# A graph kernel: the sort's schedule in the first 45 units, its exchanges partly in PSUM, and single rows in every block

## The chip, the cores and the metric

One core of a Trainium2 chip runs the whole program. The metric is device time in microseconds, from one launch to its end. TensorE (PE) multiplies, VectorE (DVE), ScalarE (ACT) and GpSimd (POOL) work element by element, SyncE (SP) only issues transfers. POOL also issues the indirect transfers, in which each of 128 partitions fetches or writes one row at an address that it holds itself.

## What is computed

The input is `x`, 12500 nodes of 256 features, with two graphs on it. With `ln` for the layer norm over features:

```
x1  = x  + (segment_sum(ln(x)[src] * edge_weight, dst) @ W.T + b)     # 200000 edges, sorted by dst
h   = ln(x1) @ W_gat                      # 16 numbers per node: 4 heads x 4 experts
att = softmax over the edges into each node of leaky_relu(a_src[src] + a_dst[dst])
                                          # 131072 unsorted edges and a loop per node
scores = mean over heads of ln(segment_sum(h[src] * att) + b_gat) * gamma + beta
w   = softmax over the best 2 of the 4 experts, 0 for the others
out = x1 + sum over experts e of w[e] * (gelu(ln(x1) @ W1[e] + b1[e]) @ W2[e] + b2[e])
```

## The kernel before

All is float32. The kernel has four parts: `layernorm_and_plan` (the normalised rows and a plan of steps), `weighted_sums`, `attention_and_experts` and `combine`. The change touches the second and the third.

**weighted_sums** (lines 504 to 1128). The 200000 edges stand in 1563 columns of 128, four columns to a group, 391 groups. POOL fetches the source rows of a group with four indirect gathers (L712) into one of the 16 slots of the ring `rows`; before it refills a slot it waits until TensorE has done the last step on the group that lies there. A step (L881) multiplies one group with one-hot matrices that VectorE writes (L938 and L942, into a ring of 4 steps), and adds to the sums of one tile of 128 nodes in PSUM. There are 488 steps: one for each group, and one more for each tile end inside a group. The destinations are dense at low node numbers (`dst` is 12500 times the square of a uniform number), so early steps seldom end a tile and late ones often do. At a tile's end TensorE runs `stages` (L859 to L873), and ScalarE takes the results out of PSUM.

Beside the steps VectorE sorts the 131072 edges of the second graph by destination, and counts them. The order is written out by hand: the loop over steps is cut into 60 units of 8 steps, and between the loops of two units stand pieces of the sort (`sort_at`), histogram pieces (`hist_at`), and on TensorE the histogram's matmuls and transposes of the keys (`TURN_AT`).
- The sort is bitonic, with keys of 128 partitions by 1024 columns. Inside a partition it is done by `exchange`: the smaller and the larger of the elements that differ in one bit of the column number, in two operations from one SBUF buffer into another (L987, L988). There are 153 exchanges in 24 stretches (pieces 0 to 23). Between stretches 9 to 23 TensorE transposes the keys into the PSUM tensor `turned`, and VectorE copies them out (L1000).
- A histogram piece takes 32 compares on VectorE (L1059) and 16 matmuls on TensorE. There are 64. The buffers hold two, so that VectorE waits for the matmuls of the piece two before.

The table gives the last unit that holds each thing, before and after the change. It follows from the table of numbers in the code:

| | before | after |
|---|---|---|
| first transpose of keys | unit 15 | unit 11 |
| last exchange, end of the sort | unit 51 | unit 45 |
| last histogram piece | unit 49 | unit 42 |
| units with no sort and no histogram behind the last transpose, to unit 59 | 52 to 59 | 46 to 59 |

After the last step the terms of the nodes are computed (L1093 to L1107), and POOL spreads the destinations' terms to the first edge of each node (L502), 28 of 98 tiles here and the others in the next part.

**attention_and_experts** (lines 1130 to 1618). TensorE runs the experts' matmuls (L1369, L1380) for 49 pairs of tiles. Beside them the attention runs over the 1024 sorted edge columns in eight blocks, the last one of 44 columns and the others of 140. A column of a block is fetched by one indirect gather on POOL (L1286), except its last two columns in the first seven blocks: these SP fetches with 256 transfers of one row each (`single_rows`, L1253), whose addresses it reads out of SBUF (`ask`, L1239). VectorE computes a block between the work of fixed pairs, and the last block behind them.

## Time and profile before

| | us |
|---|---|
| three timed runs | 3705.07, 3705.21, 3710.14 (median 3705.21) |
| the profiled execution | 3709.83 |
| its span in the trace | 3708.0 |

The span lies 1.8 us under the device time of the same execution, and that execution is 4.6 us above the median of the three.

| engine | busy us | share |
|---|---|---|
| PE | 3033.7 | 82% |
| POOL | 2700.9 | 73% |
| DVE | 2035.0 | 55% |
| ACT | 819.2 | 22% |

Shares over the whole span hide that the stages have different limits. `weighted_sums` lasts until about 2115 us, `attention_and_experts` from there to about 3531 us, and `combine` takes the rest. Each must be read by itself.

### The profile page before, as it was taken

To read this page: it belongs to the slowest core of one execution; us is meant where nothing else is said; L and a number is where in the kernel's file an instruction comes from. 1 tells how busy PE (TensorE), PEld (TensorE's weight loads), DVE (VectorE), ACT (ScalarE), POOL (GpSimd) and SP (SyncE) were. 2 spreads that over 40 slices of the span, in tenths; PEclk is the share of its full clock that TensorE was granted. 3 is DMA by queue.
4 is the path that set the end of the run, shared out by engine and by line. 5 is a ranking of instruction groups with operands and counts; after the bars stand their busy time and mean duration, and the time that the engine had idled before them with its cause. 6 is when DMAs were issued, how large, how long until landed. Compare 5 with 4: busy or idle time off the path is not lost. (4 is left out here: it accounts for less than half of the span.)

```text
span 3708.0 us, 65908 instructions
## 1 busy us (share of the span) xinstructions
PE 3033.7 (82%) x13893; PEld 2476.2 (67%) x13894; DVE 2035.0 (55%) x6854; ACT 819.2 (22%) x2321; POOL 2700.9 (73%) x2803
## 2 busy tenths in 40 slices
PE   1666667667777777887899799999999999999748
PEld 1454445555565555665677588888888888888637
DVE  8875566576667767666664322353434343343567
ACT  6300000100111111111122222222332223222247
POOL 6677777777777777777677477777777777777573
PEclk6788887887888878788899899999999999999979
DMA  9633333434444444444344122232322222223279
GB/s 346 209 115 105 108 108 110 115 113 114 117 118 114 118 118 120 118 124 118 106 125 133 51 72 54 53 112 63 75 57 73 54 72 60 73 54 75 65 281 381
DMA packets 280932, 426.20 MB, mean 115 GB/s; under 512 B 63672, under 2 KB 214499, under 8 KB 279651
## 3 DMA queue, kind: packets, MB, share of 16 engines
q0 software_dynamic: 113760, 216.95, 23.2%
q1 hardware_dynamic: 68911, 114.88, 8.5%
q10 hardware_dynamic: 98004, 91.50, 7.6%
q8 instruction: 93, 1.52, 0.2%
q14 instruction: 164, 1.34, 0.1%
HBM read 317.12 MB, written 105.98 MB: 114 GB/s over the span
## 5 line engine op out<-in xcount | busy, mean ns | idle before, releaser
L712 POOL DMA_INDIRECT rows<-feats,src_t x1500 | 1459.6, 973 | 484.0 <-issue 453.5
L881 PE MATMUL node_sums<-rows,ys_ahead 128*128 x3904 | 1063.5, 432 | 479.7 <-DVE ys_ahead L942 244.8
L881 PEld LDWEIGHTS node_sums<-rows,ys_ahead 128*128 128x128 f32 x3904 | 817.0, 216 | 683.9 <-issue 550.2
L1286 POOL DMA_INDIRECT got<-row_dram,src_sorted x1010 | 977.2, 968 | 308.1 <-issue 308.1
L1369 PE MATMUL d_hidden<-d_yt,w 128*128 128x256 f32 x3136 | 711.2, 380 | 0.8 <-DVE d_yt L1455 0.8
L1380 PE MATMUL d_expert<-w,hid 128*128 128x256 f32 x3136 | 708.7, 379 | 0.0
L1380 PEld LDWEIGHTS d_expert<-w,hid 128*128 128x128 f32 x3136 | 595.8, 190 | 81.0
L1369 PEld LDWEIGHTS d_hidden<-d_yt,w 128*128 128x128 f32 x3136 | 593.7, 191 | 80.3 <-DVE d_yt L1455 1.2
L1432 DVE TENSOR_TENSOR yo<-d_expert,x_and_b 128x512 f32<-128x512 f32 x196 | 135.5, 691 | 839.8 <-PE d_expert L1380 832.2
L942 DVE TENSOR_SCALAR ys_ahead<-iota,rel,ew_t 128x128 f32<-128x128 f32 x1952 | 557.2, 361 | 66.4 <-DVE rel L938 3.8
L1313 ACT ACTIVATE hid<-d_hidden,b1c 128x256 f32<-128x256 f32 x784 | 324.4, 471 | 982.5 <-PE d_hidden L1369 793.4
L771 ACT COPY edge_plan<-node_sums 128x256 f32<-128x256 f32 x98 | 36.5, 373 | 1665.0 <-PE sums_and_xc_turned L873 1665.0
L938 DVE TENSOR_SCALAR rel<-dst_t,step_base 128x4 f32 x488 | 125.7, 258 | 473.2 <-PE node_sums L881 330.3
L1059 DVE TENSOR_SCALAR ys_ahead<-iota_b,hist_columns 128x128 bf16<-128x128 bf16 (+1 forms) x2048 | 333.4, 281 | 2.3
L502 POOL DMA_INDIRECT adst_first<-node_dst,first_pos x98 | 97.0, 990 | 66.3 <-DVEq L1106 36.7
L1712 POOL DMA_INDIRECT edge_plan<-state_dram,last_pos x98 | 96.0, 980 | 31.8 <-issue 29.6
L869 PE MATMUL x_product<-edge_plan 128*128 128x256 f32 x400 | 114.2, 412 | 0.0
L1783 PE MATMUL f_sum<-ys,gate_diagonals 128*128 128x256 f32 x384 | 89.4, 393 | 22.7 <-issue 11.6
L1783 PEld LDWEIGHTS f_sum<-ys,gate_diagonals 128*128 128x128 f32 x384 | 74.6, 197 | 37.1 <-issue 26.4
L1055 DVE CAST hist_columns<-ys_ahead 128x16 f32<-128x16 bf16 x128 | 17.3, 186 | 147.3 <-PE counts L893 140.2
L869 PEld LDWEIGHTS x_product<-edge_plan 128*128 128x128 f32 x400 | 83.6, 209 | 13.7
L346 POOL DMA_INDIRECT rows<-in_x,src_t x64 | 61.9, 967 | 34.1 <-issue 19.2
(303 smaller groups left out, 2315.0 us busy)
## 6 DMA issues: line engine op xcount, KB each, us to landing
y_dram<-yo ACTq DMA_DIRECT2D x196, 256.0 KB
ys<-y_dram SPq DMA_DIRECT2D x36, 1024.0 KB, 9.2
got<-row_dram SPq DMA_DIRECT2D x1792, 0.1 KB
rows<-feats,src_t POOLq DMA_INDIRECT x1500
got<-row_dram,src_sorted POOLq DMA_INDIRECT x1010, 2.4
ys_ahead<-y_dram SPq DMA_DIRECT2D x13, 1024.0 KB, 9.1
x_dram<-edge_plan ACTq DMA_DIRECT2D x98, 128.0 KB
d_x<-x_dram ACTq DMA_DIRECT2D x49, 256.0 KB
```

What stands on the lines that cost most here:

```text
L712: pool.indirect_dma_start(rows[:, g % RING, j, :], None, feats, bass.IndirectOffsetOnAxis(ap=m.src_t[:, g * GT + j:g * GT + j + 1], axis=0 ...
L869: t = pe.matmul(psX[:, 0:FEAT], sums_t[:, k * P:(k + 1) * P], w_t[:, k, :], start=False, stop=(k == HALVES - 1))
L881: t = pe.matmul(psA[:, ds(((code >> 1) & 1) * 512, FEAT)], hot[:, r, j, :], rows[:, ds((code >> 2) & (RING - 1), 1), j, :], start=False, s ...
L938: v.tensor_scalar(rel[:, r, :], m.dst_t[:, ds(g * GT, GT)], m.step_base[:, ds(s, 1)], None, ALU.subtract).then_inc(s_rel, 1)
L942: t = v.tensor_scalar(hot[:, r, j, :], m.iota[:], rel[:, r, j:j + 1], m.ew_t[:, ds(g * GT + j, 1)], ALU.is_equal, ALU.mult)
L1059: c.inc(v.tensor_scalar(t[:, q % 2, j, :], iota_b[:, 0:wide], col[:, q % 2, n, j:j + 1], None, ALU.is_equal))
L1286: pool.indirect_dma_start(got[:, k, j, 0:ROWF], None, m.row_dram, bass.IndirectOffsetOnAxis(ap=m.src_sorted[:, BEGIN[b] + j:BEGIN[b] + j + ...
L1313: t = act.activation(hid[:, e % 2, 2 * q + f, :], psL[(e % 2) * 2 + q][:, f, :], ACT.Gelu, bias=b1c[:, e, 2 * q + f:2 * q + f + 1])
L1369: t = pe.matmul(psL[(e % 2) * 2 + q][:, f, :], w1[:, h, e, (2 * q + f) * P:(2 * q + f + 1) * P], yt[:, k, h, :], start=(h == 0), stop=(h = ...
L1380: q = pe.matmul(psO[e % 2][:, t, :], hid[:, e % 2, f, t * P:(t + 1) * P], w2[:, f, e, :], start=(f == 0), stop=(f == FB - 1))
L1432: v.tensor_tensor(yo[:, e, :, :], psO[e % 2][:], xb[:, e, :, :], ALU.add).then_inc(s_yo, 1)
L1783: q = pe.matmul(psum[j % SUMS][:, t, :], diag[:, j % DIAGS, t, e, :], y_of(i)[:, t, e, :], start=(e == 0), stop=(e == EXPERTS - 1))
```

## The change

Three edits.

1. The table of the sort's pieces and of the histogram's. A stretch of up to 7 exchanges is no longer cut in two (before: up to 5), short stretches share a unit up to 6 exchanges, and a unit takes two histogram pieces whenever its exchanges are at most 4 (before: only in a unit with a transpose).
2. `exchange` makes four operations of half the size where it made two. The elements whose next bit is one are written to the PSUM tensor `turned` instead of SBUF, so that the next exchange has one input in SBUF and one in PSUM. Only the first exchange of each of the 24 stretches has both inputs in SBUF. The exchange of bit 0 stays at two operations and writes SBUF only.
3. The last block too gets its last two columns from SP. SP fetches the single rows of block 0 before it waits for the 98 spread tiles and loads `adst`.

```diff
-            half = bits_of(n) if bits_of(n) <= 5 else (bits_of(n) + 1) // 2
+            half = bits_of(n) if bits_of(n) <= 7 else (bits_of(n) + 1) // 2
...
-            u += n >= 9
+            u += 2 * (n >= 9)
...
-            more = min(HPIECES - q, 2 if n in TURN_AT else 1)
+            more = min(HPIECES - q, 1 if sum(z - a for _, a, z in sort_at.get(n, [])) > 4 else 2)
...
+            def upper(bit):
+
+                n = bit % 2 * (GCOLS // 2)
+                return psT[:, n:n + GCOLS // 2].rearrange("p (a w) -> p a w", w=1 << bit)
+
-            def exchange(buf, bit):
+            def exchange(buf, bit, first):
+
                 to = 1 if buf == 2 else 1 - buf
                 a = key[buf].rearrange("p (a h w) -> p a h w", h=2, w=1 << bit)
                 o = key[to].rearrange("p (a h w) -> p a h w", h=2, w=1 << bit)
-                c.inc(v.tensor_tensor(o[:, :, 0, :], a[:, :, 0, :], a[:, :, 1, :], ALU.min))
-                c.done(v.tensor_tensor(o[:, :, 1, :], a[:, :, 0, :], a[:, :, 1, :], ALU.max))
+                x, y = a[:, :, 0, :], a[:, :, 1, :] if first else upper(bit)
+                if bit == 0:
+                    c.inc(v.tensor_tensor(o[:, :, 0, :], x, y, ALU.min))
+                    c.done(v.tensor_tensor(o[:, :, 1, :], x, y, ALU.max))
+                    return to
+                half = 1 << (bit - 1)
+                u = upper(bit - 1).rearrange("p (a h) w -> p a h w", h=2)
+                for side, op in ((0, ALU.min), (1, ALU.max)):
+                    c.inc(v.tensor_tensor(o[:, :, side, 0:half], x[:, :, 0:half], y[:, :, 0:half], op))
+                    c.inc(v.tensor_tensor(u[:, :, side, :], x[:, :, half:2 * half], y[:, :, half:2 * half], op))
+                v.wait_ge(s_s, c.n)
                 return to
...
-        single = lambda b: SINGLE if b < BLOCKS - 1 else 0
...
             ask(0)
+            single_rows(0)
             sp.wait_ge(m.s_sc, 16 * TILES)
             sp.dma_start(adst[:], m.adst_first[0:GEDGES, :].rearrange("(p j) h -> p j h", p=P)).then_inc(s_ad, 16)
-            single_rows(0)
             for b in range(BLOCKS):
-                if b + 1 < BLOCKS - 1:
+                if b + 1 < BLOCKS:
                     ask(b + 1)
                     single_rows(b + 1)
```

VectorE at the end of the sort, before: these operations stand behind the steps of unit 51. `seg_keep` and `src_sorted` are the two key buffers in SBUF, and the numbers are the partitions and the shape of the output.

```order
L987 TENSOR_TENSOR src_sorted<-seg_keep 128x128x4
L988 TENSOR_TENSOR src_sorted<-seg_keep 128x128x4
L987 TENSOR_TENSOR seg_keep<-src_sorted 128x256x2
L988 TENSOR_TENSOR seg_keep<-src_sorted 128x256x2
L987 TENSOR_TENSOR src_sorted<-seg_keep 128x512
L988 TENSOR_TENSOR src_sorted<-seg_keep 128x512
L1019 TENSOR_SCALAR seg_keep<-src_sorted 128x1024
```

After the change the same exchanges stand behind the steps of unit 45. `turned` is the PSUM tensor.

```order
L1002 TENSOR_TENSOR src_sorted<-seg_keep,turned 128x128x2
L1003 TENSOR_TENSOR turned<-seg_keep,turned 128x128x2
L1002 TENSOR_TENSOR src_sorted<-seg_keep,turned 128x128x2
L1003 TENSOR_TENSOR turned<-seg_keep,turned 128x128x2
L1002 TENSOR_TENSOR seg_keep<-src_sorted,turned 128x256
L1003 TENSOR_TENSOR turned<-src_sorted,turned 128x256
L1002 TENSOR_TENSOR seg_keep<-src_sorted,turned 128x256
L1003 TENSOR_TENSOR turned<-src_sorted,turned 128x256
L996 TENSOR_TENSOR src_sorted<-seg_keep,turned 128x512
L997 TENSOR_TENSOR src_sorted<-seg_keep,turned 128x512
L1035 TENSOR_SCALAR seg_keep<-src_sorted 128x1024
```

Two operations over 512 elements have become four over 256, except the last exchange, and each has one input in SBUF and one in PSUM. In all VectorE gets 258 operations more, two for each of 129 exchanges.

SP at the start of `attention_and_experts`, before: the index load, the load of `adst`, and then the first single rows.

```order
L1239 DMA edge_plan<-src_sorted 1x128x2
L1259 DMA adst<-adst_first 128x4096
L1248 TENSOR_LOAD edge_plan
L1253 ISA
L1253 DMA got<-row_dram 1x20
```

After the change the single rows of block 0 (now L1268) stand between the two, and `adst` (now L1275) is followed by the index load of block 1:

```order
L1268 ISA
L1268 DMA got<-row_dram 1x20
L1275 DMA adst<-adst_first 128x4096
L1254 DMA edge_plan<-src_sorted 1x128x2
L1263 TENSOR_LOAD edge_plan
```

The 256 transfers have moved ahead of the load of `adst`.

## Rows read from the trace of the kernel before

**Rows 1.** The page's costliest groups: busy us, mean ns of one, idle before.
```profile
L712 POOL DMA_INDIRECT rows<-feats,src_t x1500 | 1459.6, 973 | 484.0 <-issue 453.5
...
L1059 DVE TENSOR_SCALAR ys_ahead<-iota_b,hist_columns 128x128 bf16<-128x128 bf16 (+1 forms) x2048 | 333.4, 281 | 2.3
```

**Rows 2.** Windows of L712 alone, POOL's gathers: busy us (x instructions), clock, DMA.
```profile
0.00:1682.00 1682.00, 1195.11 (x1228) 0.83 0.45 133
```

**Rows 3.** Windows of L938 alone, one operation of VectorE per step.
```profile
0.00:1682.00 1682.00, 96.99 (x373) 0.83 0.45 133
1890.00:2087.00 197.00, 16.41 (x64) 1.00 0.38 112
```

**Rows 4.** Windows of L859 alone, four matmuls per tile end.
```profile
0.00:1682.00 1682.00, 41.70 (x244) 35.69 (x244) 0.83 0.45 133
1890.00:2087.00 197.00, 13.05 (x85) 11.01 (x85) 1.00 0.38 112
```

**Rows 5.** Waits of PE from 220 to 1000 us: total us, times, longest.
```profile
PE node_sums L881 <- SPq L696: 163.2, 69, 7.9
```

**Rows 6.** Waits of PE from 1000 to 1890 us.
```profile
PE node_sums L881 <- DVE ys_ahead L942: 140.9, 19, 8.5
PE node_sums L881 <- SPq L696: 50.0, 9, 8.4
```

**Rows 7.** Waits of PE from 1890 to 2090 us, the whole answer.
```profile
PE node_sums L881 <- issue: 0.6, 2, 0.4
```

**Rows 8.** Waits of POOL from 1730 to 1900 us.
```profile
POOL rows L712 <- PE node_sums L881: 18.3, 8, 6.8
```

**Rows 9.** Windows of L712 over the 38 stretches of exchanges, sum of all.
```profile
sum 205.30, POOL 159.84; mean POOL 4.21
```

**Rows 10.** Timeline of DVE, inputs in SBUF and PSUM (e_turn).
```profile
2123.87 0.41 DVE L1439 TENSOR_TENSOR x_and_b<-d_x,e_turn 128x256 f32<-128x256 f32 x1
2124.31 0.42 DVE L1441 TENSOR_TENSOR x_and_b<-d_x,e_turn 128x256 f32<-128x256 f32 x1
2124.65 0.41 DVE L1439 TENSOR_TENSOR x_and_b<-d_x,e_turn 128x256 f32<-128x256 f32 x1
```

**Rows 11.** Timeline of POOL in the experts' part.
```profile
3442.59 0.94 POOL L1286 DMA_INDIRECT got<-row_dram,src_sorted  x1 [0.30 <-issue]
3443.84 1.15 POOL L1286 DMA_INDIRECT got<-row_dram,src_sorted  x1 [0.30 <-issue]
```

**Rows 12.** Timeline of DVE at the same place.
```profile
3442.56 0.69 DVE L1432 TENSOR_TENSOR yo<-d_expert,x_and_b 128x512 f32<-128x512 f32 x1 [4.84 <-PE d_expert L1380]
...
3443.74 0.42 DVE L1441 TENSOR_TENSOR x_and_b<-d_x,b2r 128x256 f32<-128x256 f32 x1
```

**Rows 13.** Timeline of POOL at the end of the gathers.
```profile
2045.57 0.95 POOL L712 DMA_INDIRECT rows<-feats,src_t  x1 [0.30 <-issue]
2083.25 1.78 POOL L502 DMA_INDIRECT adst_first<-node_dst,first_pos  x1 [36.73 <-DVEq L1106]
```

**Rows 14.** Timeline of PE at the last step.
```profile
2083.07 3.72 PE L881 MATMUL node_sums<-rows,ys_ahead 128*128 x16
```

**Rows 15.** Windows of all engines in the experts' part: PE, PEld, DVE, ACT, POOL.
```profile
2200.00:2300.00 100.00, 100.00 (x471) 88.05 (x470) 27.08 (x55) 23.19 (x56) 75.90 (x80) 1.00 0.30 74
```

**Rows 16.** Timeline of SP at the start of the experts' part.
```profile
2116.73 0.55 SPq L1239 DMA_DIRECT2D edge_plan<-src_sorted  x1
2212.29 0.33 SPq L1259 DMA_DIRECT2D adst<-adst_first  x1
2213.62 134.46 SPq L1253 DMA_DIRECT2D got<-row_dram  x256
```

**Rows 17.** Line L1467, the first use of adst: ns min/median/max, first and last start.
```profile
L1467 DVE TENSOR_TENSOR_SCAN adst<-seg_keep,adst x4: 2283/2285/2293, 2335.3 to 2356.2; 128x1024 f32<-128x1024 f32 x4
```

**Rows 18.** Timeline of DVE where the last block begins.
```profile
3507.74 0.18 DVE L1478 TENSOR_SCALAR limit<-seg_keep 128x44 f32<-128x44 f32 x1 [0.23 <-DVE last_state L1515]
```

More of the change, by code:

```diff
@@ L608, in weighted_sums @@
         for n in range(PIECES):
-            half = bits_of(n) if bits_of(n) <= 5 else (bits_of(n) + 1) // 2
+            half = bits_of(n) if bits_of(n) <= 7 else (bits_of(n) + 1) // 2
             for a in range(0, bits_of(n), half):
-                sort_at[u] = (n, a, min(a + half, bits_of(n)))
-                u += 1
-            last_of.append(u - 1)
-            u += n >= 9
+                if sort_at.get(u) and sum(z - y for _, y, z in sort_at[u]) + min(half, bits_of(n) - a) > 6:
+                    u += 1
+                sort_at.setdefault(u, []).append((n, a, min(a + half, bits_of(n))))
+            last_of.append(u)
+            u += 2 * (n >= 9)
         TURN_AT = {last_of[n] + 1: n - 9 for n in range(9, PIECES - 1)}
@@ L993, in columns @@
                 for bit in range(bits_of(n) - 1 - a, bits_of(n) - 1 - z, -1):
-                    buf = exchange(buf, bit)
+                    buf = exchange(buf, bit, first=bit == bits_of(n) - 1)
                 return buf
@@ L1123, in _ @@
                     sort_init()
-                if n in sort_at:
-                    buf = sort_piece(*sort_at[n], buf)
+                for piece in sort_at.get(n, []):
+                    buf = sort_piece(*piece, buf)
                 if n == SORTED:
@@ L1206, in attention_and_experts @@
         size = lambda b: BEGIN[b + 1] - BEGIN[b]
-        single = lambda b: SINGLE if b < BLOCKS - 1 else 0
-        in_quarter = lambda b, q: max(0, min(size(b) - single(b), (q + 1) * QUARTER) - q * QUARTER)
+        in_quarter = lambda b, q: max(0, min(size(b) - SINGLE, (q + 1) * QUARTER) - q * QUARTER)
         rows_of = lambda b: got[:, b % NBUF, 0:size(b), :]
@@ L1284, in _ @@
                     pool.wait_ge(s_kept[k], b // NBUF * 16)
-                for j in range(size(b) - single(b)):
+                for j in range(size(b) - SINGLE):
                     pool.indirect_dma_start(got[:, k, j, 0:ROWF], None, m.row_dram,
@@ L1475, in maxima @@
                         v.wait_ge(s_got[b % NBUF][q], 16 * sum(in_quarter(a, q) for a in range(b % NBUF, b + 1, NBUF)))
-                if single(b):
-                    v.wait_ge(s_single, 16 * (1 + SINGLE * P) * (b + 1))
+                v.wait_ge(s_single, 16 * (1 + SINGLE * P) * (b + 1))
                 c.done(v.tensor_scalar(limit[:, 0:n], m.seg_keep[:, j], 2 * BIG, -BIG, ALU.mult, ALU.add))
```

## Prediction

> **What bounds the kernel now.** I read the 40 slices first, then windows over each part. In the experts' part TensorE is busy all the time, at the full clock (2.4 GHz), while POOL is at 76% and VectorE at 27% [rows 15]. No edit takes work from TensorE there, so I looked for the gain in `weighted_sums`, which ends near 2115 us.
>
> There two chains run side by side. POOL must issue 1500 gathers. One takes 973 ns and 0.30 us of issue, 1.27 us together, or 5.1 us for a group of four [rows 1]. VectorE and TensorE must work off the groups. Up to 1000 us TensorE waits 163 us for rows [rows 5]: POOL is the slower chain. From 1000 to 1890 us it waits only 50 us for rows but 141 us for one-hot matrices that VectorE, busy with the sort and the histogram, delivers late [rows 6]. So here the pair falls behind. At 1682 us, where unit 46 begins, POOL has issued (64+1228)/4 = 323 groups (the 64 gathers of the first ring included), and VectorE has begun 373 steps at 244/4 = 61 tile ends, which is group 311 [rows 2 to 4]. The lead is 12 of the 16 slots. Soon after, the ring is full: POOL waits 18.3 us in all for TensorE between 1730 and 1900 us, in 8 waits [rows 8].
>
> From 1890 us on there is neither sort nor histogram, and TensorE waits for nothing [rows 7]. The last gather ends at 2046.5 us, the last step at 2086.8 us, 40 us later; POOL sits idle for 36.7 us until it may spread the terms [rows 13, 14]. So the pair's work sets the end, and everything after moves with it.
>
> **The cost of an exchange.** Now 153 exchanges fill 205.3 us [rows 9], 1.34 us each. Four operations of 256 elements with one input in PSUM: the trace has such operations, and the next one starts 0.34 us later where nothing is waited for, and 0.44 us later behind a wait [rows 10]. Three by 0.34 plus 0.44 is 1.46 us, so 0.12 us more per exchange, and 15 us of VectorE time over 129 exchanges. The lower end is 1.34, as now. No row shows VectorE writing PSUM. The upper end is four operations that each take as long as one of 512 elements now, 0.67 us: 2.68 us. I take 1.46, from the rows with the same size and the same inputs; that a write to PSUM costs what one to SBUF does is my assumption.
>
> The Trainium skill speaks against this edit. Its page VectorE: DVE Perf Modes, section The TRN2 errata, gives a fixed 58 cycles for an operation from SBUF and 120 for one from PSUM, 65 ns more. By that an exchange would take 1.7 us and the forecast would be some 8 us later. The rows do not show that difference.
>
> **What an exchange does to POOL.** The 38 stretches of exchanges last 205.3 us, in which POOL is busy 159.8 us [rows 9]. The 45.5 us left, at 0.30 us a gather, are some 150 gathers of 1.07 us, where an undisturbed gather lasts 0.95 and the next starts after 1.25 us (3442.59 to 3443.84 [rows 11]), which would make 164. So the exchanges hold POOL up by 14 gathers, 18 us. In the experts' part the same is seen in single operations: the gather that starts beside `yo`, which reads PSUM and SBUF, takes 0.94 us, and the one beside `x_and_b<-d_x,b2r`, which reads SBUF twice, takes 1.15 us [rows 11, 12]. With 129 of 153 exchanges no longer reading SBUF twice I take back 129/153 of 18, 15 us. The bounds are 0 and 18 us.
>
> Here the Trainium skill has another view. Its page SBUF — State Buffer, section Who interferes with whom, says that `tensor_tensor` takes only the pair's read interface while descriptor generation needs the write interface (it marks this as inferred). By that the 15 us are zero. The gathers of 1.07 us contradict it here.
>
> **The pair's chain, after.** Up to unit 27 (near 1050 us) TensorE waits for rows anyway, and the denser units use those 163 us; I cost that at nothing. Without this cover the ring would be full earlier, and each further us of work would be one at the end. From there to unit 46 the new table has 62 exchanges instead of 55, and 23 histogram pieces instead of 25. In VectorE time: 62 by 1.46 less 55 by 1.34 is +17 us. Two histogram pieces fewer, at 333.4/64 = 5.2 us [rows 1] and about 1 us around them, -12 us. The end of the sort, nine or so operations over 1024 elements, and two more copies out of PSUM: an estimate of +13 us, scaled from the 512-element operations. Together +18 us. TensorE's steps run beside part of VectorE's work, so I put half on the path, +9: unit 46 starts at 1691 us (0 to 18 bound it: 1682 to 1700).
>
> From there 80 groups remain, 311 to 390, with no sort and no histogram. Their price is what the end of the trace shows: from 1890 us to the last step 64 one-hot sets are begun, and TensorE has two or three steps still to do at the start; less 85/4 = 21 tile ends [rows 3, 4] that is about 46 groups in 197 us, 4.3 us a group. 80 by 4.3 is 344 us, so the last step ends at 2035 us.
>
> **POOL's chain, after.** It has to be checked, because it may be the later of the two. The last gather ended at 2046.5. Less 15 us (exchanges) and less 16 us (the 18.3 of waits, less 8 by 0.30 of ordinary issue) it ends at 2015 us. Landing, a step and the tile ends around it add 6 to 10 us: 2023 us. The pair's chain is later, and the two terms on POOL do not add to the gain; they are what lets the pair run on without a wait.
>
> So the last step moves from 2086.8 to 2035, -52 us. The tail behind it (four tile ends, the last terms, the spreads) is unchanged.
>
> **The edits at nothing.** SP loads `adst` behind 256 single rows, 134.5 us [rows 16]. Before, the load went out at 2212.3 because it waits for the 98 spreads; now it goes out some 136 us after the first index load at 2116.7, so at 2253 us on the old scale, 40 us later. Its first use is at 2335.3 [rows 17]. About 70 us of cover are left. What is queued behind it on SP, the next index load and single rows, comes no later than before. In the last block POOL saves two gathers, 2.5 us, but VectorE begins that block right behind its own last operation, idle for 0.23 us [rows 18], so nothing is won; SP's 256 rows for it go out beside the pairs before. Zero for both.
>
> **Sum.** Profiled span 3708.0 - 52 = 3656 us, and with the 1.8 us around it 3658. The median stands 4.6 us under the profiled execution: 3653 us, 1.4% faster. A difference of 0.2% (7.4 us) is what a measurement of this kernel can tell from none.
>
> **Rivals.**
> - *The ring fills in the middle.* If the added work falls wholly on the path, or TensorE's clock, 0.83 on the mean up to 1682 us [rows 2], stays low in the denser units, the ring is full before unit 46 and POOL stands as it did at 1730 us. The lead of 12 slots of 16 at 1682 us speaks for it: 4 slots are 20 us. The price is +9 for the half that I left off the path and 10 to 20 us of POOL's standing. 3675 us.
> - *POOL is the bound.* If the pair gets through the last 14 units at less than 4.3 us a group (units 46 to 50 end fewer tiles than the last ones), the floor of 2023 us counts: -64 us, 3641 us. Against it: in supply-bound stretches the clock was lower, and the pair slower.
> - *PSUM brings nothing to POOL.* Then POOL's chain ends 15 us later, at 2038, about level with the pair's, and each disturbs the other a little: 3660 us. [rows 11, 12] speak against it.
> - *Writing PSUM is dear* (the slow side). An exchange of 2.68 us adds 1.22 us to each of 62 exchanges from 1050 us on, all on the path once the pair is the bound: +76 us against -52, so 3705 + 24 = 3729 us. It decides from 2.3 us an exchange on, where 62 times the excess eats the 52. Only the missing row speaks for it, and that ScalarE and TensorE also use PSUM then.
>
> **Chances.** Forecast 0.50 (3645 to 3667); ring fills 0.17; POOL bound 0.12; PSUM without gain 0.08; PSUM dear 0.07; the rest, such as a new wait in the order of transposes and histogram pieces, 0.06, half of it slower or same. The range reaches from the POOL bound, 3638, to a full ring at its dearest, 3690. Faster 0.87, within 0.2% 0.05, slower 0.08.
>
> **What would show it.** Exchanges: operations of 0.41 us that follow each other by 0.34. POOL: gathers beside them at 0.95 us, and no waits for TensorE around 1750 us. The pair: a lead of 12 slots or more at the start of unit 46, near 1690 us, shrinking to a few, so that the last step follows the last gather by some 20 us and not 40. The experts' part: as long as before, TensorE at 100%. The forecast is wrong if the lead reaches 16 before unit 40, if an exchange takes over 1.6 us, or if VectorE waits at the first use of `adst`.

## The result, and the profile after

| | us |
|---|---|
| before, four runs | 3705.07 to 3710.14, median 3706.56 |
| after, four runs | 3660.9 to 3672.25, median 3666.07 |
| ratio | 0.989, 95% interval 0.9869 to 0.9911 |
| profiled execution after | 3672.25, span 3670.3, mean clock 0.897 |

The change makes the kernel 1.1% faster. The forecast was 3653 us with a range from 3638 to 3690: right in its sign and inside the range, 13 us too low.

Two lines of the page after: the gathers, and the operation of VectorE with which each histogram piece begins (busy us, mean ns of one, idle before, and what ended most of it).

```profile
L713 POOL DMA_INDIRECT rows<-feats,src_t x1500 | 1438.5, 959 | 495.9 <-issue 442.3
...
L1071 DVE CAST hist_columns<-ys_ahead 128x16 f32<-128x16 bf16 x128 | 17.9, 196 | 146.6 <-PE counts L894 137.6
```

Against [rows 1] the 1500 gathers last 21.1 us less (1459.6 to 1438.5, 973 to 959 ns), but the idle time ahead of them is 11.9 us longer (484.0 to 495.9). The difference of the two, 9.2 us, is nearly all of how much earlier the last gather ends: 2037.1 instead of 2046.5 us. The experts' matmuls take 380 ns, as before, and from 2200 to 2300 us TensorE is busy for all of the 100 us, as in [rows 15].

How far the pair of VectorE and TensorE stands behind POOL is counted as in [rows 2 to 4]: windows over L713 (gathers), L939 (one per step) and L860 (four matmuls per tile end), of the kernel after, from the start to the beginning of units 27, 42 and 46.

```profile
0.00:1054.00 1054.00, 715.57 (x745) 0.79 0.47 142
0.00:1579.00 1579.00, 1100.43 (x1148) 0.81 0.45 133
0.00:1699.00 1699.00, 1184.10 (x1235) 0.81 0.44 132
```

```profile
0.00:1054.00 1054.00, 55.55 (x221) 0.79 0.47 142
0.00:1579.00 1579.00, 85.97 (x340) 0.81 0.45 133
0.00:1699.00 1699.00, 94.13 (x373) 0.81 0.44 132
```

```profile
0.00:1054.00 1054.00, 15.68 (x96) 13.32 (x96) 0.79 0.47 142
0.00:1579.00 1579.00, 35.79 (x212) 30.57 (x212) 0.81 0.45 133
0.00:1699.00 1699.00, 40.74 (x244) 34.74 (x244) 0.81 0.44 132
```

At 1054 us: (64+745)/4 = 202 groups issued, 221 - 96/4 = 197 begun, a lead of 5. The same count for the kernel before, at its unit 27, has two rows (L712, L938) and the same 24 tile ends:

```profile
0.00:1047.00 1047.00, 711.59 (x732) 0.81 0.47 141
```

```profile
0.00:1047.00 1047.00, 56.90 (x220) 0.81 0.47 141
```

(64+732)/4 = 199 less 196 is 3. At 1579 us after: 303 issued, 340 - 53 = 287 begun. The lead is 16, the ring is full. At 1699 us it is 325 - 312 = 13. The same count on [rows 2 to 4] gives 323 - 312 = 11 at unit 46 before; the 12 of the prediction takes the group by its number, which starts at 0.

The windows end where a unit begins, so they also give the time of each stretch (the last two rows are read from their traces in the same way):

| us | to unit 27 | units 27 to 45 | unit 46 to the end of the last step | sum |
|---|---|---|---|---|
| before | 1047 | 635 | 405 | 2087 |
| forecast | 1047 | 644 | 344 | 2035 |
| after | 1054 | 645 | 350 | 2049 |
| table alone (h1_schedule) | 1052 | 647 | 349 | 2048 |
| histogram earlier (f1_hist_early) | 1072 | 583 | 368 | 2023 |

Waits of TensorE from 220 to 1000 us, and from 1000 to 1890 us (total, times, longest):

```profile
PE node_sums L882 <- DVE ys_ahead L943: 182.8, 21, 14.0
PE node_sums L882 <- SPq L697: 91.8, 22, 13.9
```

```profile
PE node_sums L882 <- DVE ys_ahead L943: 155.2, 22, 13.8
PE node_sums L882 <- SPq L697: 11.3, 4, 7.9
```

By these lines the waits for rows before 1000 us fell from 163.2 [rows 5] to 91.8 us, and those for VectorE rose to 182.8 us. Before the change the same stretch had for VectorE:

```profile
PE node_sums L881 <- DVE ys_ahead L942: 82.0, 14, 8.4
```

From 1000 to 1890 us they stand at 11.3 us for rows and 155.2 for VectorE, against 50.0 and 140.9 [rows 6].

These lines put a wait down to the semaphore that moved last before it, and here that is wrong for the long ones. A step really waits for rows in the first of these two places, and for VectorE in the second:

```profile
472.46 0.94 POOL L713 DMA_INDIRECT rows<-feats,src_t  x1 [0.30 <-issue]
475.71 0.48 PE L882 MATMUL node_sums<-rows,ys_ahead 128*128 x1 [2.97 <-SPq L697]
```

```profile
351.46 1.11 DVE L943 TENSOR_SCALAR ys_ahead<-iota,rel,ew_t 128x128 f32<-128x128 f32 x4
353.19 1.22 PE L882 MATMUL node_sums<-rows,ys_ahead 128*128 x2 [13.94 <-SPq L697]
```

At 475.71 TensorE starts 2.3 us behind the last gather of the step's group, and the one-hot matrices have been ready for 7 us. At 353.19 it starts 0.6 us behind the last one-hot matrix, and the rows were fetched 22 us before. Sorted by these two distances, step by step, the waits for rows from 220 to 1000 us are 149 us before and 33 us after, and those for VectorE 93 and 240 us. From 1000 to 1890 us the waits for rows are 3 us before and none after. So up to unit 27 the denser units used up most of the time in which TensorE had waited for rows, and the pair of VectorE and TensorE sets the pace behind it in both kernels.

Waits of POOL for TensorE, first in all, then the two longest, each in the brackets of the gather that it held up:

```profile
POOL rows L713 <- PE node_sums L882: 53.5, 48, 9.6
```

```profile
1485.83 0.94 POOL L713 DMA_INDIRECT rows<-feats,src_t  x1 [9.60 <-PE node_sums L882]
...
1523.03 0.94 POOL L713 DMA_INDIRECT rows<-feats,src_t  x1 [7.12 <-PE node_sums L882]
```

It was 30.5 us in all before, and the part of it in [rows 8] lay behind 1730 us. The first wait of the ring lasts 9 to 10 us in both kernels, but the page before puts it down to issue: behind 200 us the sums are 29.3 us before and 43.7 us after. Now POOL stands again and again from 1476 us, the start of the wait of 9.6 us, up to 1620 us, in units 39 to 43. It waits for TensorE, and VectorE may be four steps ahead of TensorE, so POOL stands already at a lead of 12 or so, counted as above.

The waits of TensorE from unit 46 to the last step (1699 to 2050 us), and the one long one among them:

```profile
PE node_sums L882 <- DVE ys_ahead L943: 9.8, 2, 9.5
PE node_sums L882 <- SPq L697: 0.2, 1, 0.2
```

```profile
1700.82 3.78 PE L882 MATMUL node_sums<-rows,ys_ahead 128*128 x8 [9.54 <-DVE ys_ahead L943]
```

This wait is for the last exchanges and the end of the sort on VectorE. Behind it TensorE runs without a pause to the last step. It waits 0.2 us for rows: the pair still sets the end, and not POOL.

The end of the first part, on POOL and on TensorE:

```profile
2036.19 0.95 POOL L713 DMA_INDIRECT rows<-feats,src_t  x1 [0.30 <-issue]
2044.98 1.77 POOL L502 DMA_INDIRECT adst_first<-node_dst,first_pos  x1 [7.84 <-DVEq L1122]
```

```profile
2044.95 3.72 PE L882 MATMUL node_sums<-rows,ys_ahead 128*128 x16
```

Against [rows 13, 14], the last gather is 9 us earlier, the last step ends at 2048.7 instead of 2086.8 us, 38 us earlier, and POOL is idle for 7.8 instead of 36.7 us before it spreads. That is the whole gain: from the end of the last step to the end of the span it takes 1621.2 us before and 1621.6 after.

| us | last gather ends | last step ends | from there to the end of the span |
|---|---|---|---|
| before | 2046.5 | 2086.8 | 1621.2 |
| after | 2037.1 | 2048.7 | 1621.6 |
| table alone (h1_schedule) | 2037.8 | 2047.5 | 1619.0 |
| histogram earlier (f1_hist_early) | 2017.5 | 2023.3 | 1622.7 |

VectorE in three exchanges that follow each other, after (start, duration):

```profile
238.28 0.42 DVE L1002 TENSOR_TENSOR src_sorted<-seg_keep,turned 128x256 f32<-128x256 f32 x1
238.61 0.42 DVE L1003 TENSOR_TENSOR turned<-seg_keep,turned 128x256 f32<-128x256 f32 x1
...
239.28 0.42 DVE L1003 TENSOR_TENSOR turned<-seg_keep,turned 128x256 f32<-128x256 f32 x1
239.73 0.63 DVE L1002 TENSOR_TENSOR seg_keep<-src_sorted,turned 128x256 f32<-128x256 f32 x1
240.26 0.62 DVE L1003 TENSOR_TENSOR turned<-src_sorted,turned 128x256 f32<-128x256 f32 x1
...
241.29 0.62 DVE L1003 TENSOR_TENSOR turned<-src_sorted,turned 128x256 f32<-128x256 f32 x1
241.94 0.69 DVE L996 TENSOR_TENSOR src_sorted<-seg_keep,turned 128x512 f32<-128x512 f32 x1
```

Two operations of another exchange of bit 1, the first of its stretch, with both inputs in SBUF:

```profile
140.83 0.63 DVE L1002 TENSOR_TENSOR seg_keep<-src_sorted 128x256 f32<-128x256 f32 x1
141.36 0.62 DVE L1003 TENSOR_TENSOR turned<-src_sorted 128x256 f32<-128x256 f32 x1
```

And a gather of POOL beside the first exchange:

```profile
238.94 0.95 POOL L713 DMA_INDIRECT rows<-feats,src_t  x1 [0.30 <-issue]
```

The first four operations are an exchange as forecast, 0.42 us each and 0.33 us apart, and a gather beside them takes 0.95 us; the next follows by 1.25. The next four are the exchange of bit 1. Each of its operations takes single elements, every fourth one of a key buffer in SBUF and every second one in PSUM. Each takes 0.62 us and starts 0.52 us after the last: 2.2 us for the exchange. The row at 140.83 shows that PSUM is not the reason: it neither reads nor writes it and takes as long. The last row of the first list is bit 0, two operations of 512 elements, every second one of a key buffer, and takes the same 0.69 us as in the kernel before.

### The profile page after: what moved, and what is told of

It reads as the page before. It is cut to its first block and busy times, and to the rows that moved or that the text cites. A ratio compares the mean times of both kernels' runs of the same rounds, so it can differ in the third digit from the quotient of the medians.

```text
span 3670.3 us, 66961 instructions
## 1 busy us (share of the span) xinstructions
PE 2976.7 (81%) x13893; PEld 2447.2 (67%) x13894; DVE 2067.3 (56%) x7112; ACT 817.7 (22%) x2321; POOL 2677.2 (73%) x2801
## 5 line engine op out<-in xcount | busy, mean ns | idle before, releaser
L713 POOL DMA_INDIRECT rows<-feats,src_t x1500 | 1438.5, 959 | 495.9 <-issue 442.3
L882 PE MATMUL node_sums<-rows,ys_ahead 128*128 x3904 | 1019.7, 420 | 499.1 <-DVE ys_ahead L943 377.3
L882 PEld LDWEIGHTS node_sums<-rows,ys_ahead 128*128 128x128 f32 x3904 | 796.8, 210 | 683.3 <-issue 555.4
L939 DVE TENSOR_SCALAR rel<-dst_t,step_base 128x4 f32 x488 | 122.1, 250 | 403.1 <-PE node_sums L882 267.5
L502 POOL DMA_INDIRECT adst_first<-node_dst,first_pos x98 | 96.3, 983 | 37.4 <-issue 29.3
L1797 PE MATMUL f_sum<-ys,gate_diagonals 128*128 128x256 f32 x384 | 89.3, 393 | 22.6 <-issue 11.8
L1071 DVE CAST hist_columns<-ys_ahead 128x16 f32<-128x16 bf16 x128 | 17.9, 196 | 146.6 <-PE counts L894 137.6
```

Source lines behind the costliest of these rows:

```text
L713: pool.indirect_dma_start(rows[:, g % RING, j, :], None, feats, bass.IndirectOffsetOnAxis(ap=m.src_t[:, g * GT + j:g * GT + j + 1], axis=0 ...
L882: t = pe.matmul(psA[:, ds(((code >> 1) & 1) * 512, FEAT)], hot[:, r, j, :], rows[:, ds((code >> 2) & (RING - 1), 1), j, :], start=False, s ...
L939: v.tensor_scalar(rel[:, r, :], m.dst_t[:, ds(g * GT, GT)], m.step_base[:, ds(s, 1)], None, ALU.subtract).then_inc(s_rel, 1)
L1797: q = pe.matmul(psum[j % SUMS][:, t, :], diag[:, j % DIAGS, t, e, :], y_of(i)[:, t, e, :], start=(e == 0), stop=(e == EXPERTS - 1))
```

## Experiments

Each kernel differs from the one named by the diff that stands there. Two of them, and the two kernels of the case, were timed in the condition of the profile above. The other ten ran where the kernel before itself takes 5921 to 5985 us; they are compared with the kernel before in that same condition alone, and have a section of their own below, since TensorE stands there for long stretches. It is not a matter of the chip alone: h1_schedule and h2_psum ran on the same one, the first beside a kernel before of 3705 us, the second beside one of 5985 us.

### The table alone (h1_schedule)

The kernel before, with only the first edit:

```diff
-            half = bits_of(n) if bits_of(n) <= 5 else (bits_of(n) + 1) // 2
+            half = bits_of(n) if bits_of(n) <= 7 else (bits_of(n) + 1) // 2
...
-            u += n >= 9
+            u += 2 * (n >= 9)
...
-            more = min(HPIECES - q, 2 if n in TURN_AT else 1)
+            more = min(HPIECES - q, 1 if sum(z - a for _, a, z in sort_at.get(n, [])) > 4 else 2)
```

> The kernel before with the change's table of steps and gathers alone (denser first 45 units, single rows in all eight blocks); exchanges all in SBUF, SyncE's edit and the last block's order as before. Theory A (the table brings the whole gain, the exchange in PSUM only shifts work between VectorE and POOL): 3660 to 3675 us, the last gather at 2030 to 2045 us, TensorE's last node-sum step within 15 us behind it, gathers at a mean of 970 to 975 ns. Theory B (the gain needs the gathers freed of VectorE's two-input operations): 3690 to 3706 us, the last gather behind 2055 us.

Measured: 3673.64 us (3664.35 to 3676.49, 5 runs), ratio 0.9912 [0.9899, 0.9926]. The last gather ends at 2037.8, the last step at 2047.5 us, 10 us behind it. That is Theory A, but for the mean of a gather, 969 ns where it said 970 to 975. The expectation speaks of single rows in all eight blocks too; they belong to the third edit, which this kernel leaves out. The page's lines for the gathers and for the start of each histogram piece, and POOL's waits for TensorE:

```profile
L713 POOL DMA_INDIRECT rows<-feats,src_t x1500 | 1452.8, 969 | 482.2 <-issue 440.5
...
L1056 DVE CAST hist_columns<-ys_ahead 128x16 f32<-128x16 bf16 x128 | 17.8, 190 | 178.8 <-PE counts L894 168.0
```

```profile
POOL rows L713 <- PE node_sums L882: 41.7, 54, 8.9
```

So the table brings 0.9% by itself, and the whole change 1.1% [0.9, 1.3]; the intervals overlap. That the exchange in PSUM adds anything is not shown. What it does is seen between these two traces: it makes the gathers 14.3 us shorter (1452.8 to 1438.5) and VectorE's busy time 29.4 us longer (2037.9 to 2067.3), and POOL waits 11.8 us more for TensorE (41.7 to 53.5). The last gather ends 0.7 us earlier: what POOL gained it gave back at the ring. VectorE's longer work did not move the pair either. Unit 46 begins at 1698.5 and at 1698.7 us: VectorE waits 30 us less for the histogram's matmuls (168.0 to 137.6), about as much as its exchanges take longer.

That the inputs in SBUF hold the gathers up is seen gather by gather. In this kernel 133 gathers overlap exchange operations alone, all with both inputs in SBUF, and take 1.07 us on the mean. In the changed kernel 144 overlap only exchange operations with one input in PSUM and take 0.95 us, as the gathers do beside an idle VectorE. Of the 21 us by which the whole change shortens the gathers, 14 come with the exchange and 7 with the table (1459.6 to 1452.8).

### The histogram earlier (f1_hist_early)

The changed kernel, with two histogram pieces in each of the units 1 to 17 and from there as in the kernel before. The histogram then ends in unit 38 instead of 42.

```diff
-            more = min(HPIECES - q, 1 if sum(z - a for _, a, z in sort_at.get(n, [])) > 4 else 2)
+            more = min(HPIECES - q, 2 if 1 <= n < 18 or n in TURN_AT else 1)
```

> The changed kernel, but the histogram's pieces stand earlier: two in each of the units 1 to 17 and in the units with a transpose, one in the others. 35 pieces instead of 27 are done by unit 17, and 29 instead of 37 remain. In the changed kernel TensorE waits 92 us for rows between 220 and 1000 us, and POOL waits for TensorE 53 us in all, mostly from 1490 to 1690 us with a full ring. Theory A (the middle, units 18 to 42, is bound by VectorE and TensorE together, 34 us a unit against 31 us of gathers): eight pieces by some 8 us leave the middle and go where TensorE waited for rows; the ring no longer fills, POOL's last gather moves from 2037 us to 2000 to 2010 us, and the last step follows within 15 us. Time 3630 to 3645 us. Rival (pieces cost their time wherever they stand, since the early ring too has little lead): the early lag grows instead, POOL stands before 1000 us, and the time stays at 3660 to 3672 us.

Measured: 3647.02 us (3643.04 to 3647.89, 5 runs), ratio 0.9834 [0.9821, 0.9848], the fastest of all, and clear of the changed kernel's interval. The last gather, at 2017.5 us, and the time lie just outside Theory A (2000 to 2010 us, and 3630 to 3645), and far from the rival. The line of the gathers, POOL's waits for TensorE, VectorE's waits for the matmuls of the histogram, TensorE's waits for rows from 1699 to 2050 us, and the last step:

```profile
L713 POOL DMA_INDIRECT rows<-feats,src_t x1500 | 1445.3, 964 | 469.3 <-issue 444.2
```

```profile
POOL rows L713 <- PE node_sums L882: 25.2, 43, 8.8
```

```profile
DVE hist_columns L1071 <- PE counts L894: 93.4, 24, 10.9
```

```profile
PE node_sums L882 <- SPq L697: 13.4, 10, 3.3
```

```profile
2019.54 3.72 PE L882 MATMUL node_sums<-rows,ys_ahead 128*128 x16
```

Busy and idle time of the gathers are 1914.6 us together, 19.8 less than after, and the last gather ends 19.6 us earlier. All of it is idle time (495.9 to 469.3): POOL waits 25.2 instead of 53.5 us, 8.8 of it at the very start of the ring. The gathers themselves are 6.8 us longer; I have no cause for that.

The pair gains more than that. It reaches unit 27 18 us later than in the changed kernel, with seven more histogram pieces done, and unit 46 44 us earlier (1655.0 against 1698.7). VectorE's wait for the histogram's matmuls fell by the same 44 us, from 137.6 (the page after) to 93.4. From unit 46 the part then takes 368 instead of 350 us: now TensorE waits for rows, 13.4 us in 10 waits, and the last step follows the last gather by 6 us. In this kernel POOL sets the end of the part, as the rival "POOL is the bound" has it, and the last step ends at 2023.3 us, where that rival put it (2023); only it expected this of the changed kernel.

### Ten runs where the kernel before takes 5921 to 5985 us

Here the three edits, and two variants, were tried each by itself. First what bounds the kernel in this condition, from the trace of e3_sp, which takes as long as the kernel before. Two rows of TensorE in the experts' part, one behind the other, and lines of its page:

```profile
4020.32 0.58 PE L1379 MATMUL d_expert<-w,hid 128*128 128x256 f32 x1 [2.23 <-issue]
4023.11 0.58 PE L1379 MATMUL d_expert<-w,hid 128*128 128x256 f32 x1 [2.21 <-issue]
```

```profile
L712 POOL DMA_INDIRECT rows<-feats,src_t x1500 | 1443.5, 962 | 1287.8 <-PE node_sums L881 720.1
...
L1368 PE MATMUL d_hidden<-d_yt,w 128*128 128x256 f32 x3136 | 803.8, 398 | 529.3 <-issue 527.5
...
L1055 DVE CAST hist_columns<-ys_ahead 128x16 f32<-128x16 bf16 x128 | 17.4, 190 | 425.0 <-remote 283.8
```

The matmuls of `d_hidden`, idle for 0.8 us in all in the normal condition, wait 527.5 us here for nothing that the profile shows. Where they do, as in these rows, TensorE starts one matmul every 2.8 us, and the operation itself takes 0.58 us. The mean clock is 0.74 against 0.90. In the first part TensorE is the slower chain all along, POOL waits 720.1 us for it, and the last gather ends at 2867 us. Why it is so the traces don't tell.

The expectations of these runs were written for the condition in which the kernel before takes 3706 us, and the theories in them that concern `weighted_sums` are not decided here.

**The table alone, twice** (e1_schedule, g1_schedule; the diff of h1_schedule).

> Only the new table of sort and histogram pieces; exchanges as before (two operations, both inputs in SBUF), SP's order and the last block as before. Theory A (what pays is that units 46 to 59 hold no sort, so that the steps catch up with the gathers; the gathers' own speed matters only while the ring is not full): VectorE has some 30 us less to do than in the changed kernel, so the ring fills later and POOL waits less for TensorE than the 53 us of the changed kernel, but a gather stays at about 973 ns, 20 us more over all. The two nearly cancel: last gather at 2030 to 2045 us, last step within 15 us of it, 3660 to 3675 us in all. Theory B (the PSUM exchange is what pays): 3690 to 3706 us.

> Only the new table; exchanges as before, SP's order and the last block as before. In a first measurement on another chip every kernel, the unchanged one too, ran at about 5980 us, and TensorE stood some 3.6 us before each loop body; this is the same kernel on a chip where the unchanged one takes 3706 us. Theory A (units 46 to 59 without sort let the steps catch up; the gathers' speed matters only while the ring is not full): VectorE has some 30 us less to do than in the changed kernel, a gather stays at 973 ns, 20 us more over all, and the two nearly cancel: last gather at 2030 to 2045 us, the last step within 15 us of it, 3660 to 3675 us. Theory B (the exchange in PSUM is what pays): 3690 to 3706 us.

Measured: 6082.4 us (before 5980.4), 1.0177 [1.0158, 1.0196]; and 6004.4 (before 5921.1), 1.014 [1.0117, 1.0162]. The same edit that brings 0.9% above costs 1.4 to 1.8% here. The page of e1_schedule, the gathers and the first operation of the histogram pieces:

```profile
L713 POOL DMA_INDIRECT rows<-feats,src_t x1500 | 1447.1, 965 | 1358.0 <-PE node_sums L882 810.3
...
L1056 DVE CAST hist_columns<-ys_ahead 128x16 f32<-128x16 bf16 x128 | 17.0, 182 | 537.4 <-remote 334.2
```

VectorE's idle time before the histogram pieces is 537.4 us against 425.0 in e3_sp, and the last gather ends at 2943 instead of 2867 us. The page names no releaser ("remote") for 334.2 us of it, but by the code VectorE waits there only for the histogram's matmuls. A likely cause is that with two pieces in one unit VectorE meets buffers that the slow TensorE has not read yet, and that the next steps wait behind VectorE. The 112 us of longer waits and the 76 us of a longer part have the same sign; no run takes the second piece away by itself, so this cause is not shown.

**The exchange alone, three times** (e2_psum, g2_psum, h2_psum): the kernel before with the second edit, as in the section on the change. The expectation of h2_psum speaks of 38 exchanges; 38 is the number of stretches between steps in the kernel before, and the edit changes 129 exchanges.

> Only the exchange in four operations with PSUM; table and SP as before. Theory A: gathers fall to about 959 ns, but VectorE has 30 us more to do in a stretch where steps and VectorE already lag; the ring fills before unit 47, POOL gives the 20 us back by standing, and the last step still follows the last gather by some 40 us: 3705 to 3722 us, the same or slower. Theory B: 15 to 20 us faster, 3687 us.

> Only the exchange in four operations with PSUM. Theory A: gathers fall to about 959 ns, VectorE has 30 us more to do, the ring fills before unit 47, POOL gives the 20 us back by standing, and the last step still follows the last gather by some 40 us: 3705 to 3722 us. Theory B: 15 to 20 us faster, 3687 us.

> The kernel before with the exchanges of next bit one in PSUM alone (four operations each, 38 exchanges); table of steps and gathers as before. The middle of the first part is set by VectorE and TensorE there, and POOL waits 36.7 us behind its last gather. Theory A (half of the exchanges' extra work lies on the path): 13 exchanges at 1.46 instead of 1.34 us and bit 1's at 2.2 us give 18 to 35 us more of VectorE, gathers at a mean of 958 to 963 ns give back to POOL what it has to spare already, so 3705 to 3722 us. Theory B (freeing the gathers is worth its whole 20 us by itself): about 3687 us.

Measured: 1.0034 [1.0018, 1.005], 1.0034 [1.0016, 1.0053], 1.003 [1.0017, 1.0044] (6001.4, 5942.0 and 5999.8 us). So 15 to 21 us longer, each time. The gathers are shorter here too:

```profile
L712 POOL DMA_INDIRECT rows<-feats,src_t x1500 | 1437.8, 959 | 1305.4 <-PE node_sums L881 731.6
```

This is e2_psum; e3_sp beside it has 1443.5 us, 962 ns. That is 6 us on an engine that waits 700 us anyway. That what VectorE has more to do lies on the path would explain the 15 to 21 us, but is not shown. What this edit alone does where the kernel takes 3706 us was not measured.

**SyncE's rows and the last block alone** (e3_sp).

```diff
+            single_rows(0)
             sp.wait_ge(m.s_sc, 16 * TILES)
             sp.dma_start(adst[:], ...)
-            single_rows(0)
...
-                if b + 1 < BLOCKS - 1:
+                if b + 1 < BLOCKS:
```

> Only the edits on SP and the last block: single rows of block 0 before the load of adst, two gathers fewer in the last block. Theory A and the prediction's step: zero, 3706 us within 5; VectorE does not wait at the first use of adst. Rival: the load of adst, 40 us later, holds the experts' part up, and the time is over 3715 us; or the last block's two gathers were on the path, and it is 2 to 3 us faster.

Measured: 5986.47 us, 1.0003 [0.999, 1.0016]. Zero, as forecast. In the normal condition h1_schedule, which lacks this edit, needs 1619.0 us behind its last step and the changed kernel 1621.6: no gain there either.

**Bit 1 in two operations** (e4_bit1, g4_bit1, h3_bit1): the changed kernel, with the exchange of bit 1 in two operations of 512 elements. They still read one input in PSUM, where the exchange before has put it, but write both halves to SBUF, so that bit 0 reads SBUF twice.

```diff
-                x, y = a[:, :, 0, :], a[:, :, 1, :] if first else upper(bit)
-                if bit == 0:
+                x, y = a[:, :, 0, :], a[:, :, 1, :] if first or bit == 0 else upper(bit)
+                if bit <= 1:
```

> The changed kernel, but the exchange of bit 1 makes two operations over 512 elements, one input in SBUF and one contiguous in PSUM, and writes both halves to SBUF; the exchange of bit 0 then reads SBUF twice. In the changed kernel the four operations of bit 1 take 0.62 us each against 0.42 of the others, 2.2 us for the exchange. Theory A: bit 1 falls to 1.34 us, 0.85 by 22 exchanges is 19 us less of VectorE, the lag of the steps at unit 40 shrinks by 10 to 15 us, POOL stands less, and the time falls by 8 to 14 us, to 3652 to 3658 us. Rival (the middle is set by TensorE and the histogram, not by the exchanges): no change, 3666 us.

> The changed kernel with the exchange of bit 1 in two operations over 512 elements, one input in SBUF and one contiguous in PSUM, both halves written to SBUF; bit 0 then reads SBUF twice. Theory A: bit 1 falls from 2.2 to 1.34 us, 19 us less of VectorE in all, the lag at unit 40 shrinks by 10 to 15 us and POOL stands less: 3652 to 3658 us. Rival (the middle is set by TensorE and the histogram, not by the exchanges): 3666 us.

> The changed kernel, but the exchanges with the elements of bit 1 (22 in blocks 1 to 7; four operations of 0.62 to 0.63 us in the changed kernel's trace, 2.2 us each) are made in two operations of 512 elements with both halves in SBUF, as in the kernel before (1.34 us each). That takes 16 to 19 us from VectorE before the last gather. Theory A (VectorE's work in the middle fills the ring of gathered rows around units 40 to 44, and POOL's halt there carries through to the end): POOL waits less for TensorE between 1000 and 1700 us (34.5 us in the changed kernel), the last gather ends at 2022 to 2032 instead of 2037 us, and the time is 3654 to 3663 us. Theory B (these 16 us lie beside POOL's own chain): the last gather stays within 3 us of 2037 and the time within 3 us of 3666; with 22 exchanges' gathers held again by 0.1 us each it could be 2 to 4 us longer.

Measured: 1.0217 [1.0197, 1.0237], 1.0201 [1.0182, 1.0221], 1.0227 [1.0209, 1.0246] (6114.5, 6039.1 and 6108.5 us). The exchange of bit 1 itself costs what was expected, two operations of 0.69 and 0.68 us in e4_bit1. On the time they tell nothing: the changed kernel itself was not run in this condition, so there is nothing to set them against. An estimate from the table (+1.4 to 1.8%) and the exchange (+0.3%) puts it at 1.017 to 1.021, and the three are at that or up to 0.3% above. The variant stays open in the normal condition.

**Histogram earlier and bit 1 in two operations** (g5_hist_early_bit1): both diffs above.

> The earlier histogram together with bit 1 in two operations. The earlier histogram alone took 3647 us. Theory A: if POOL still stood for TensorE there, the cheaper bit 1 takes that away too, and 3637 to 3645 us follow; if POOL no longer stood, its 1500 gathers are the bound, and bit 0, which reads SBUF twice again, costs 2 to 4 us of gathers: 3647 to 3651 us. Rival: the gains add in full, 3647 less 10, 3637 us or below, though POOL did not wait.

Measured: 6073.7 us, 1.0266 [1.0246, 1.0286], slower than g4_bit1 beside it. The earlier histogram costs 0.6% in this condition (VectorE's idle time before its pieces is 603.8 us here, 552.4 in g4_bit1), while in the normal one f1_hist_early is the fastest kernel. Its expectation stays open.

## Why the prediction was right, and where not

**Forecast against trace.** The profiled execution was forecast at 3658 us and took 3672.25. The last step was forecast to end at 2035 and ended at 2048.7 us. The 14 us are the same in both, so the miss lies ahead of the last step and nowhere else.

**The path.** That the pair's work behind unit 46 sets the end, and that the denser units pull it forward, was right. From unit 46 to the end of the last step the part takes 350 us instead of 405, while the units ahead take 17 us more: that is the gain of 38 us. TensorE waits 0.2 us for rows there. h1_schedule has the table alone and shows the same. The middle was right too: from unit 27 to 46 it is 10 us more, forecast were 9. That "half on the path" came out so well is partly luck. The prediction counts 25 histogram pieces before in these units, and the table of the code gives 26, which takes 6 us from its sum of VectorE's work; eight exchanges of bit 1 in them, each 0.75 us dearer than it had them, put as much back.

**The step that was off** is "up to unit 27 TensorE waits for rows anyway; I cost that at nothing". The cover was there and was used: of 149 us of real waits for rows 33 are left. But VectorE's added work stands in lumps between two units, and TensorE waits for VectorE at the first step of the next one, mostly 8 to 14 us at a time. Unit 27 began 7 us later than before. The other half of the miss is the price of a group in the last stretch, 350 us for 344. Taken step by step, a group costs 4.4 us there after the change and 4.4 us in the same stretch of the kernel before; the forecast had 4.3 from its windows. The 79 groups left (not 80: the count from 0 again) make 348 us, and TensorE begins 2 us behind VectorE.

**The mark for "wrong".** The prediction called itself wrong if the lead reached 16 before unit 40. By the count it reaches 16 at unit 42, and it is 14 at the start of unit 40. But POOL's first halt ended at 1486 us, ahead of unit 40's start at 1507, at a lead of 12: the mark did not allow for the steps that VectorE is ahead. So the ring did fill in the middle, as that rival has it. Its price did not come, though. The rival adds 10 to 20 us for POOL's standing, and nothing of it can be at the end, since TensorE has its rows from unit 46 on. That the result (3666) lies between the forecast (3653) and the rival (3675) is chance.

**The exchange.** 1.46 us was right for the exchanges of bit 2 and above, for writes to PSUM too. Missed was bit 1, 2.2 us: 22 exchanges by 0.75 are 16 us of VectorE on top of the 15 that the forecast had. The pages show 29.4 us more between h1_schedule and the changed kernel. By the prediction's own mark, over 1.6 us, this is a sign of being wrong, met by 22 of the 129 changed exchanges; it cost nothing that can be seen, since VectorE waited as much less elsewhere. The 120 cycles that the Trainium skill gives for PSUM in VectorE: DVE Perf Modes, section The TRN2 errata, are not seen in these rows: with inputs in SBUF and PSUM and 256 elements an operation takes 0.41 to 0.42 us here, wherever it writes, and with both inputs in SBUF 0.42 us too, bit 1 aside.

**POOL.** That two inputs in SBUF hold the gathers up was right in its mechanism: forecast 15 us, measured 14.3 between h1_schedule and the changed kernel, and 6 us between e3_sp and e2_psum. The remark in the section Who interferes with whom of the Trainium skill's page SBUF — State Buffer that `tensor_tensor` leaves descriptor generation alone, which it marks as inferred, and by which the 15 us would be zero, is contradicted by the gathers of 1.07 us beside two inputs in SBUF and 0.95 us beside one. The same section also says that an instruction of VectorE with two SBUF inputs contends with one of GpSimd that reads SBUF, and one with a single SBUF input does not; with that the trace agrees, and the prediction left it out. The other term on POOL failed: the waits for TensorE were to go (-16 us) and grew by 14 behind the start, so the last gather ended at 2037 and not at 2015 us. It did not matter, since the pair's chain is the later one, as forecast. "The two terms on POOL do not add to the gain" was right.

**The lag at the end.** The last step ends 12 us behind the last gather instead of 40; forecast were 20. The lead has nearly run out by then, but POOL has not become the bound. It is close to it: when f1_hist_early lets the pair reach unit 46 44 us earlier, only 25 us of that arrive at the last step, and POOL's chain takes the rest.

**The edits at nothing.** SP and the load of `adst`, after, and the first operation of the last block:

```profile
2083.95 134.09 SPq L1268 DMA_DIRECT2D got<-row_dram  x256
2219.19 0.37 SPq L1275 DMA_DIRECT2D adst<-adst_first  x1
```

```profile
3469.75 0.19 DVE L1492 TENSOR_SCALAR limit<-seg_keep 128x44 f32<-128x44 f32 x1 [0.26 <-DVE last_state L1529]
```

`adst` is loaded at 2219.2, its first use is at 2297.3 us: 78 us of cover (forecast about 70; its own times, 2335 less 2253, make 82). VectorE begins the last block 0.26 us after its own last operation, as in [rows 18]. Both were zero.

## What to carry to other kernels

Cut the part into stretches at places that both kernels have, and give each its own time: the total hid that the first stretch and the last were 7 and 6 us off and the middle one was right. A full ring costs the producer time, but the end only moves with it if the consumer later waits for the producer; look for that wait. Before a line of waits is believed, check one long wait against the end of both things that it could wait for: here 58 of 92 us that the view puts down to rows were waits for VectorE. Before an exchange pattern is cut into smaller operations, look at its smallest stride by itself.

## What was not expected

- VectorE's operations on 256 single elements, every fourth of a buffer in SBUF: 0.62 us, against 0.42 us with runs of two or more elements, whether the other input is in SBUF or PSUM. With 512 elements, every second one, an operation takes 0.69 us, as long as with runs. That it is the distance of four elements is an inference from these rows; no run tries distances by themselves.
- With the same table, VectorE's 29 us of added exchange work did not delay unit 46 at all. It waited as much less for the histogram's matmuls.
- The same program takes 1.6 times as long in one condition (3706 and 5921 to 5985 us), with TensorE starting one matmul in 2.2 to 2.9 us for stretches of the experts' part. There the change's first edit has the other sign.
